# Gelu images of a Fourier mixer transformed as half precision pairs, written in place, with the low part formed on GpSimd

## The chip, the cores and the metric

The kernel runs on one core of a Trainium2 chip. The metric is the device time of one execution in microseconds; lower is better. The engines are TensorE (PE; weight loads are shown as PEld), VectorE (DVE), ScalarE (ACT), GpSimd (POOL) and the DMA queue of SyncE (SP). Each runs its own list of instructions in order; semaphores (`wait_ge`, `then_inc`) are all that ties them together.

## The reference, cut to what matters

The input is 4 x 32 images of 128 x 128 in float32. A Fourier neural operator layer (group norm, attention over tokens with spectral convolutions, two spectral mixer layers) is followed by a token attention and a mixture of experts. The change lies in the first mixer layer and in what feeds the second:

```python
m = instance_norm(attn, norm2_g, norm2_b)
m = fno_layer(m, mixer_w1, mixer_skip_w1, mixer_skip_b1, (H, W), norm=(mixer_norm_g1, mixer_norm_b1), act=_gelu)
m = fno_layer(m, mixer_w2, mixer_skip_w2, mixer_skip_b2, (H, W), norm=(mixer_norm_g2, mixer_norm_b2))
out = instance_norm(m, mixer_out_g, mixer_out_b) + attn
```

`fno_layer` adds a spectral convolution (forward transform, a product with weights on a few modes, inverse transform) to a pointwise skip path. So the gelu images of the first mixer layer are needed three times: their statistics, their forward transform for the second spectral convolution, and they themselves for the second skip path.

## The kernel before

There are 128 images; each lies in SBUF as 128 partitions (rows) by 128 elements. `m.b` holds the residual images, `m.a` a second set of images. `build` calls twelve stages in order, and each is a block with a barrier at its end. The change is in `stage_inverse(..., 'mix1')`, which the trace shows from about 328 to 446 us after its coefficients are turned and split; `stage_mixer` follows it and reads `m.half17` (the half transformed gelu images) and `m.stat`.

In `stage_inverse` the images are taken in 33 sets of up to 4 (`image_sets`, loop variable `b`; `width(b)` is 4 but for the last three sets, with 3, 3 and 2). Three sets form a quad `q` of 12 images, and `j` = 0, 1, 2 is the set's place in it. The engines' lists in 'mix1', per set:

- TensorE: `second(b)`, three half precision products that give the spectral rows of set b in a PSUM bank; `forward(b-2)`, for each image one float32 product of the gelu image (as weights) with the 34 columns of `dft17`, L1186; after each third set `first(q+2)`, twelve narrow half precision products for a later quad.
- VectorE: `linear(b+1)`, one tensor_scalar for each image from `m.b` into `m.tmp` (two places), L1296; it waits until the gelu of set b-1 has read its place. Then `combine(b)`, which adds the bank to `m.tmp`, L1330; `gelu_statistics(b-1)`, L1312; after each third set `half(q+2)`, L1281, the low part of the quad's half inverse, behind ScalarE's high part.
- ScalarE: the gelu of set b from `m.tmp` into the stage `m.ust` (two places, float32), L1263; `affine(b)`, which rescales the four images of `m.b` in place, L1237; `copied(b-2)`, which takes the forward product out of PSUM, L1228; after each third set `half(q+2)`, L1220.
- GpSimd: the add of the input images (loaded by SyncE into `m.a`) to `m.b`, L1142, behind `affine(b)`; then a copy of the gelu images from `m.ust` to `m.a`, L1145.
- SyncE: eleven loads of twelve images each into `m.a`, then the second mixer's weights.

The order of each list is written out by hand, as printed here:

Of the kernel before, what the change touches and what calls it, by code (L numbers as in the profile page):

```python
# [26 lines left out]
F16 = mybir.dt.float16  # L27
# [4 lines left out]
P = 128  # L32
# [138 lines left out]
def memory(nc, ctx, where):  # L171
# [3 lines left out]
    def sb(scope, name, shape, dtype=F32):  # L175
        return scope.enter_context(nc.sbuf_tensor(name, shape, dtype))
# [19 lines left out]
    with ExitStack() as l0:  # L196
        m.a = sb(l0, "images_a", [P, NI, NW])
        c0 = where['dft'][0]
        m.tab = sb(l0, "table", [P, where['var'][1] - c0])

        def tab(name, rows=P):
            lo, hi = where[name]
            return m.tab[0:rows, lo - c0:hi - c0]
        m.dft = tab('dft')
        m.dft17 = m.dft.rearrange("p (s k) -> p s k", s=2)[:, :, 0:K17]
        m.rows, m.cols, m.batch, m.low, m.var = tab('rows', FM), tab('cols', FM), tab('batch'), tab('low'), tab('var')
        pair = sb(l0, "pair", [P, 2, 2 * NM])
        m.wraw = pair[0:64, 0, :].rearrange("p (r k c) -> p r k c", r=ROWS, c=2)
        m.weff = pair[0:64, 1, :].rearrange("p (c m) -> p c m", c=2)
        m.feat = pair[:, 0, :].rearrange("p (x y) -> p x y", x=FM)  # L210
        m.coef = pair[:, 1, :].rearrange("p (x y) -> p x y", x=FM)
        mixw = sb(l0, "mixer_weights", [P, 2 * NM])
        m.mixw = mixw[:, :].rearrange("p (r k c) -> p r k c", r=ROWS, c=2)
        m.feat0 = mixw[:, :].rearrange("p (x y) -> p x y", x=FM)
        f = sb(l0, "features", [P, FQ * FQ])
        m.ft = f[:, :].rearrange("p (x y) -> p x y", x=FQ)
        m.half17 = f[:, 0:P * FM].rearrange("p (t x) -> p t x", t=P)
        g = sb(l0, "spare", [P, HC * P])
        m.spare = g[:, :]
        m.gramT = g[:, :].rearrange("p (c t) -> p c t", c=HC)  # L220
        m.coefH, m.coefL = (g[0:FM, 2 * NI * FM // 4 * i:2 * NI * FM // 4 * (i + 1)].bitcast(F16)
                            .rearrange("p (t x) -> p t x", t=NI) for i in (0, 1))
        m.modes = sb(l0, "modes", [P, 2, NM])
        r = sb(l0, "transposed", [P, 1920])
        m.turned = r[:, :]
        m.modesT = r[:, 0:1280].rearrange("p (k c t) -> p k c t", k=5, c=2)
        m.wT = r[:, 1280:1920].rearrange("p (k c h) -> p k c h", k=5, c=2)
        m.stat = r[:, 0:768].rearrange("p (t s) -> p t s", t=P)
        m.aff = r[:, 768:768 + 8 * P].rearrange("p (k t) -> p k t", k=8)
        m.halfH = sb(l0, "half_inverse_high", [P, 2, GRP * NW], F16)[0:3 * FM]  # L230
        m.halfL = sb(l0, "half_inverse_low", [P, 2, GRP * NW], F16)[0:3 * FM]
        m.rowsH = sb(l0, "rows_high", [P, 3, P], F16)[0:3 * FM]
        m.rowsL = sb(l0, "rows_low", [P, 3, P], F16)[0:3 * FM]
        m.colsH = sb(l0, "cols_high", [P, P], F16)[0:FM]
        m.colsL = sb(l0, "cols_low", [P, P], F16)[0:FM]
        m.unity = sb(l0, "unity", [P, P])[:, :]
        norms = sb(l0, "norms", [P, 160])
        m.norms = [norms[:, 32 * i:32 * i + 32] for i in range(5)]
        m.rstd, m.back = m.norms[3], m.norms[4]
        m.dftH = sb(l0, "transform_high", [P, FQ], F16)[:, :]  # L240
        m.dftL = sb(l0, "transform_low", [P, FQ], F16)[:, :]
        m.ust = shared[:, :].rearrange("p (s t w) -> p s t w", s=2, t=GRP)
        m.tmp = m.modes[:, :, 0:GRP * NW]

    b = m.b[:, :, :].rearrange("p a b -> p (a b)")
# [794 lines left out]
def stage_inverse(nc, held, m, kind, mix=None, ins=None):  # L1040


    s = semaphores(nc, held, "inverse_" + kind, "in0 in1 in2 in3 v sized rooted total scaled turned high low first bhigh "
                   "blow rows used lin ready saved forward copied weights cleared algebra affine added gstat partly")
    arrived = [s.in0, s.in1, s.in2, s.in3]
    sets = image_sets()
    up, down = m.col[:, 25:26], m.col[:, 26:27]
# [6 lines left out]
    def width(b):  # L1054
        return len(sets[b][2])
# [54 lines left out]
    with nc.Block() as block:  # L1110
# [22 lines left out]
        @block.gpsimd  # L1133
        def _(pool):
            if kind == 'proj':
                first_mixer(pool)
            if kind == 'mix1':
                for b in range(len(sets)):
                    q = sets[b][0]
                    pool.wait_ge(arrived[q % 4], 16 * (q // 4 + 1))  # L1140
                    pool.wait_ge(s.affine, b + 1)
                    pool.tensor_tensor(images(m.b, b), images(m.b, b), images(m.a, b), ALU.add).then_inc(s.added, 1)  # L1142
                    pool.wait_ge(s.added, b + 1)
                    pool.wait_ge(s.ready, b + 1)
                    pool.tensor_copy(images(m.a, b), m.ust[:, b % 2, 0:width(b)]).then_inc(s.saved, 1)  # L1145
            if kind == 'mix2':
                for b in range(len(sets)):
                    pool.wait_ge(s.lin, b + 1)
                    pool.tensor_tensor(images(m.b, b), images(m.b, b), images(m.a, b), ALU.add).then_inc(s.partly, 1)

        @block.tensor
        def _(pe):
# [26 lines left out]

            def forward(b):  # L1180

                pe.wait_ge(s.ready, b + 1)
                if b >= 2:
                    pe.wait_ge(s.copied, b - 1)
                for i in range(width(b)):
                    mm = pe.matmul(m.ps[6 + b % 2][:, i * FM:i * FM + FM], m.ust[:, b % 2, i, :], m.dft17,  # L1186
                                   start=True, stop=True)
                mm.then_inc(s.forward, 1)

            if kind == 'proj':  # L1190
# [23 lines left out]
        def _(act):  # L1214
# [7 lines left out]
                    e = act.copy(m.halfH[0:2 * FM, q % 2, whole:whole + NW], m.ps[q % 2][0:2 * FM, whole:whole + NW])  # L1222
                e.then_inc(s.bhigh, 1)

            def copied(b):
                act.wait_ge(s.forward, b + 1)
                n = width(b)
                act.copy(images(m.half17, b), m.ps[6 + b % 2][:, 0:n * FM].rearrange("p (t x) -> p t x", t=n))\  # L1228
                    .then_inc(s.copied, 1)

            def affine(b):

                q, j, gs = sets[b]
                store, k = (m.b, 0) if kind == 'mix1' else (m.a, 6)
                for i in range(len(gs)):
                    img = 12 * q + j + 3 * i
                    e = act.activation(store[:, img, :], store[:, img, :], ACT.Identity, scale=m.aff[:, k, img:img + 1],  # L1237
                                       bias=m.aff[:, k + 1, img:img + 1])
                e.then_inc(s.affine if kind == 'mix1' else s.lin, 1)
# [8 lines left out]
                act.activation(m.coefH[:, :, xs[0]:xs[0] + n], turned(r), ACT.Copy, scale=up[0:FM] if kind == 'proj' else 1.0).then_inc(s.high, 1)  # L1248
            half(0)
            half(1)  # L1250
            if kind == 'mix2':
                affine(0)
                affine(1)
            for b in range(len(sets)):
                if kind == 'mix2' and b + 2 < len(sets):
                    affine(b + 2)
                if kind == 'mix1':
                    act.wait_ge(s.used, b + 1)
                    if b >= 2:
                        act.wait_ge(s.forward, b - 1)  # L1260
                        act.wait_ge(s.saved, b - 1)
                        act.wait_ge(s.gstat, b - 1)
                    act.activation(m.ust[:, b % 2, 0:width(b)], spread(m.tmp[:, b % 2], width(b)), ACT.Gelu).then_inc(s.ready, 1)  # L1263
                    affine(b)
                    if b >= 2:
                        copied(b - 2)
                q, j, _ = sets[b]
                if j == 2 and q + 2 < QUADS:
                    half(q + 2)
            if kind == 'mix1':  # L1270
                copied(len(sets) - 2)
                copied(len(sets) - 1)

        @block.vector
        def _(vec):
# [31 lines left out]
            def gelu_statistics(b):  # L1307
                vec.wait_ge(s.ready, b + 1)
                q, j, gs = sets[b]
                for i in range(len(gs)):  # L1310
                    img = 12 * q + j + 3 * i
                    e = vec.bn_stats(m.stat[:, img, :], m.ust[:, b % 2, i, :])  # L1312
                e.then_inc(s.gstat, 1)

            def combine(b):
                vec.wait_ge(s.rows, b + 1)
# [33 lines left out]
            for b in range(len(sets)):  # L1350
                if kind == 'mix1' and b + 1 < len(sets):
                    linear(b + 1)
                combine(b)
                if b >= 1:
                    (gelu_statistics if kind == 'mix1' else statistics)(b - 1)
                q, j, _ = sets[b]
                if j == 2 and q + 2 < QUADS:
                    half(q + 2)
            (gelu_statistics if kind == 'mix1' else statistics)(len(sets) - 1)


def stage_factors(nc, held, m):
# [1135 lines left out]
```

## Time and profile before

| | |
|---|---|
| time, median of 3 runs | 2361.22 us (2359.89 to 2365.7) |
| the profiled execution's own time | 2359.8 us |
| its span | 2358.0 us |
| TensorE busy | 2084.6 us (88%) |
| VectorE busy | 1879.9 us (80%) |
| ScalarE busy | 1664.3 us (71%) |
| GpSimd busy | 601.8 us (26%) |
| mean granted TensorE clock | 0.905 of full speed |

The span is the time from the first to the last instruction; the execution's own time has 1.8 us more around it. A share of busy time is an average over twelve stages with different limits, so the stage that is changed has to be read by itself. In a timeline, neighbouring instructions of one line are merged (x4), and a bracket gives the idle time before them and what ended it; without a bracket there was practically none.

### The profile page before, as it was taken

The page shows a single profiled execution, that of the slowest core. Times are in us where ns is not written, and L with a number is a line of the kernel's source. Part 1 is how long each engine was busy: PE and PEld are TensorE (multiplying, and loading weights), DVE is VectorE, ACT ScalarE, POOL GpSimd, SP SyncE. Part 2 cuts the span into 40 slices and gives each one's busy share as a digit, 9 for nine tenths or more (in the row PEclk, how much of TensorE's full clock was granted, in tenths as well). Part 3 has the DMA queues.
Part 4 walks back from the last instruction along what each step waited for, and adds up shares of the span by engine and source line. Part 5 has one row for each costly group of instructions (what it writes and reads, how often), then busy time and mean ns, then how long its engine had stood idle before and what let it go on. Part 6 is the DMA issues. An engine that isn't in the chain of part 4 may idle for free. (4 is left out here: it accounts for less than half of the span.)

```text
span 2358.0 us, 30826 instructions
## 1 busy us (share of the span) xinstructions
PE 2084.6 (88%) x10373; PEld 1068.8 (45%) x10373; DVE 1879.9 (80%) x3566; ACT 1664.3 (71%) x2413; POOL 601.8 (26%) x751
## 2 busy tenths in 40 slices
PE   7776959874999999999999999999999999667778
PEld 7722446732444444444444444444444444323333
DVE  4667978688778888888889889888888888667776
ACT  1454236473788888888888888888888888566766
POOL 1035315345201202202202102102000000046768
PEclk9988655555999999999999999999999999788999
DMA  9003560000000000000000000000000000000101
GB/s 297 12 1 152 143 152 1 1 1 6 1 1 1 1 1 1 1 1 1 1 1 1 1 1 1 1 1 1 1 1 1 1 1 1 10 14 28 32 28 46
DMA packets 80833, 55.73 MB, mean 24 GB/s; under 512 B 11283, under 2 KB 78739, under 8 KB 79140
## 3 DMA queue, kind: packets, MB, share of 16 engines
q1 hardware_dynamic: 75476, 52.38, 7.4%
q10 hardware_dynamic: 5200, 1.38, 0.3%
q8 instruction: 83, 1.36, 0.2%
q14 instruction: 74, 0.61, 0.1%
HBM read 36.91 MB, written 16.78 MB: 23 GB/s over the span
## 5 line engine op out<-in xcount | busy, mean ns | idle before, releaser
L1912 ACT ACTIVATE inner<-banks,key_bias,scales 128x1024 f32<-128x1024 f32 x512 | 616.9, 1205 | 211.4 <-PE banks L1785 206.2
L2034 DVE TENSOR_TENSOR weights_low<-weights,weights_high 128x1024 f16<-128x1024 f32 x512 | 674.7, 1318 | 17.0
L1919 ACT ACTIVATE weights<-inner 128x1024 f32<-128x1024 f32 x512 | 541.1, 1057 | 16.1 <-DVE weights_low L2034 0.3
L2030 DVE CAST weights_high<-weights 128x1024 f16<-128x1024 f32 x512 | 371.5, 726 | 181.9 <-ACT weights L1919 169.1
L2108 POOL CAST sums_high<-sums 128x512 f16<-128x512 f32 x32 | 39.4, 1230 | 1091.3 <-ACT sums L1902 1073.3
L1785 PE MATMUL banks<-queries_high,keys_high 128*128 128x512 f16 x1024 | 304.5, 379 | 0.7 <-ACT inner L1912 0.7
L1800 PE MATMUL banks<-weights_high,tokens_low 128*128 128x512 f16 x1024 | 304.6, 379 | 0.0
L1785 PE MATMUL banks<-queries_low,keys_high 128*128 128x512 f16 x1024 | 304.6, 379 | 0.0
L1800 PE MATMUL banks<-weights_low,tokens_high 128*128 128x512 f16 x1024 | 304.5, 379 | 0.0
L1785 PE MATMUL banks<-queries_high,keys_low 128*128 128x512 f16 x1024 | 304.5, 379 | 0.0
L1800 PE MATMUL banks<-weights_high,tokens_high 128*128 128x512 f16 x1024 | 304.5, 379 | 0.0
L2289 ACT ACTIVATE scaled<-banks,gates 128x128 f32<-128x128 f32 x512 | 148.8, 394 | 85.3 <-PE banks L2236 78.8
L1800 PEld LDWEIGHTS banks<-weights_high,tokens_low 128*128 128x128 f16 x1024 | 100.2, 98 | 120.9
L1785 PEld LDWEIGHTS banks<-queries_low,keys_high 128*128 128x128 f16 x1024 | 100.2, 98 | 120.9
L1800 PEld LDWEIGHTS banks<-weights_high,tokens_high 128*128 128x128 f16 x1024 | 100.2, 98 | 120.8
L1800 PEld LDWEIGHTS banks<-weights_low,tokens_high 128*128 128x128 f16 x1024 | 100.2, 98 | 120.7
L1785 PEld LDWEIGHTS banks<-queries_high,keys_low 128*128 128x128 f16 x1024 | 100.2, 98 | 120.7
L2234 PE MATMUL banks<-expert_weights_high,normed_high 128*128 128x512 f16 x256 | 103.7, 405 | 50.3 <-DVE residual_and_scaled L2365 44.0
L1785 PEld LDWEIGHTS banks<-queries_high,keys_high 128*128 128x128 f16 x1024 | 96.9, 98 | 91.2 <-ACT inner L1912 1.7
L2429 POOL TENSOR_TENSOR scaled_halves<-scaled 128x256 f32<-128x256 f32 x128 | 93.4, 730 | 98.0 <-ACT scaled L2289 97.5
L2365 DVE SCALAR_TENSOR_TENSOR residual_and_scaled<-banks,gates,residual_and_scaled 128x128 f32<-128x128 f32 x384 | 110.0, 342 | 0.1
L2235 PE MATMUL banks<-expert_weights_low,normed_high 128*128 128x512 f16 x256 | 103.7, 405 | 0.0
(599 smaller groups left out, 3237.2 us busy)
## 6 DMA issues: line engine op xcount, KB each, us to landing
images_b<-in_x SPq DMA_DIRECT2D x32, 256.0 KB, 9.3
images_a<-in_x SPq DMA_DIRECT2D x8, 1024.0 KB, 10.3
mixed_scratch<-images_a SPq DMA_DIRECT2D x4, 2048.0 KB, 13.0
result<-group_result SPq DMA_DIRECT2D x32, 256.0 KB, 2.3
images_b<-mixed_scratch SPq DMA_DIRECT2D x10, 768.0 KB, 4.9
images_a<-in_x SPq DMA_DIRECT2D x10, 768.0 KB, 9.1
mixer_weights<-in_L_conv_mixer_w SPq DMA_DIRECT2D x4, 272.0 KB, 6.1
table<-tables ACTq DMA_DIRECT2D x1, 772.5 KB, 5.8
```

The lines of the kernel that those rows point to most:

```text
L1785: mm = pe.matmul(m.ps[2 * (t % 2) + h], key[:, par, part], query[:, q, 512 * h:512 * h + 512], start=(i == 0), stop=(i == 2))
L1800: mm = pe.matmul(m.ps[4 + h], value[:, par, k, :], weight[:, t % DEEP, 512 * h:512 * h + 512], start=(k == 0 and i == 0), stop=(k == KT - ...
L1912: act.activation(m.inner[:, t % 2, :], m.pair[t % 2], ACT.Exp, scale=m.fs[:, 1:2], bias=m.kb[:, c // QN % 2, k:k + 1]).then_inc(s.inner, 1)
L1919: act.activation(m.wt[:, t % 2, :], m.inner[:, t % 2, :], ACT.Exp).then_inc(s.outer, 1)
L2030: vec.tensor_copy(m.wH[:, t % DEEP, :], m.wt[:, t % 2, :]).then_inc(s.high, 1)
L2034: vec.tensor_tensor(m.wL[:, t % DEEP, :], m.wt[:, t % 2, :], m.wH[:, t % DEEP, :], ALU.subtract)\
L2108: after(pool.tensor_copy(m.oH[:, part], m.oS[:, part]))
L2234: pe.matmul(bank, m.lnH[:, t % RING, j, :], m.w8H[:, cols], start=True, stop=False)
L2235: pe.matmul(bank, m.lnH[:, t % RING, j, :], m.w8L[:, cols], start=False, stop=False)
L2289: o = act.activation(m.pb[:, n % 3, e, :], m.ps[ABANK[n % 2]][:, e * D:e * D + D], ACT.Copy, scale=m.gate[:, n, 4 + e:5 + e])
L2365: vec.scalar_tensor_tensor(out=m.u[:, n % 4, :], in0=m.ps[DBANK[n % 3]][:, e * D:e * D + D], scalar=m.gate[:, n, e:e + 1], in1=acc, op0=AL ...
L2429: pool.tensor_tensor(m.half[:, n % 2], m.pb[:, n % 3, 0:2], m.pb[:, n % 3, 2:4], ALU.add).then_inc(s.halved, 1)
```

## The change

The gelu image is now written to `m.a` in place of the input image (which GpSimd must have added to `m.b` before). ScalarE then copies it to half precision (`m.ustH`), GpSimd subtracts to get the low part (`m.ustL`), one set later in its list. TensorE's forward product becomes two half precision products for each image: the high part against the high and low table side by side (68 columns), and the low part against the high table (34 columns). VectorE, not ScalarE, takes the result out of PSUM and adds the two halves (`joined`), three sets later. The statistics read `m.a`. On ScalarE `affine(b+1)` now stands ahead of the gelu of set b and waits for `linear(b+1)`. The tables of the first transform, which were two tensors, lie in one.

```diff
--- before.py
+++ after.py
@@ -237,9 +237,12 @@
         norms = sb(l0, "norms", [P, 160])
         m.norms = [norms[:, 32 * i:32 * i + 32] for i in range(5)]
         m.rstd, m.back = m.norms[3], m.norms[4]
-        m.dftH = sb(l0, "transform_high", [P, FQ], F16)[:, :]
-        m.dftL = sb(l0, "transform_low", [P, FQ], F16)[:, :]
+        dfts = sb(l0, "transform_pair", [P, 2, FQ], F16)
+        m.dftH, m.dftL = dfts[:, 0, :], dfts[:, 1, :]
         m.ust = shared[:, :].rearrange("p (s t w) -> p s t w", s=2, t=GRP)
+        m.ustH, m.ustL = (shared[:, GRP * NW * i:GRP * NW * (i + 1)].bitcast(F16).rearrange("p (s t w) -> p s t w", s=2, t=GRP)
+                          for i in (0, 1))
+        m.dft17P = dfts[:, :, :].rearrange("p c (s k) -> p c s k", s=2)[:, :, :, 0:K17]
         m.tmp = m.modes[:, :, 0:GRP * NW]
 
     b = m.b[:, :, :].rearrange("p a b -> p (a b)")
@@ -1041,7 +1044,7 @@
 
 
     s = semaphores(nc, held, "inverse_" + kind, "in0 in1 in2 in3 v sized rooted total scaled turned high low first bhigh "
-                   "blow rows used lin ready saved forward copied weights cleared algebra affine added gstat partly")
+                   "blow rows used lin ready upper lower forward joined weights cleared algebra affine added gstat partly")
     arrived = [s.in0, s.in1, s.in2, s.in3]
     sets = image_sets()
     up, down = m.col[:, 25:26], m.col[:, 26:27]
@@ -1134,15 +1137,21 @@
         def _(pool):
             if kind == 'proj':
                 first_mixer(pool)
+            def below(b):
+                pool.wait_ge(s.upper, b + 1)
+                n = width(b)
+                pool.tensor_tensor(m.ustL[:, b % 2, 0:n], images(m.a, b), m.ustH[:, b % 2, 0:n], ALU.subtract)\
+                    .then_inc(s.lower, 1)
+
             if kind == 'mix1':
                 for b in range(len(sets)):
                     q = sets[b][0]
                     pool.wait_ge(arrived[q % 4], 16 * (q // 4 + 1))
                     pool.wait_ge(s.affine, b + 1)
                     pool.tensor_tensor(images(m.b, b), images(m.b, b), images(m.a, b), ALU.add).then_inc(s.added, 1)
-                    pool.wait_ge(s.added, b + 1)
-                    pool.wait_ge(s.ready, b + 1)
-                    pool.tensor_copy(images(m.a, b), m.ust[:, b % 2, 0:width(b)]).then_inc(s.saved, 1)
+                    if b:
+                        below(b - 1)
+                below(len(sets) - 1)
             if kind == 'mix2':
                 for b in range(len(sets)):
                     pool.wait_ge(s.lin, b + 1)
@@ -1179,12 +1188,13 @@
 
             def forward(b):
 
-                pe.wait_ge(s.ready, b + 1)
+                pe.wait_ge(s.lower, b + 1)
                 if b >= 2:
-                    pe.wait_ge(s.copied, b - 1)
+                    pe.wait_ge(s.joined, b - 1)
                 for i in range(width(b)):
-                    mm = pe.matmul(m.ps[6 + b % 2][:, i * FM:i * FM + FM], m.ust[:, b % 2, i, :], m.dft17,
-                                   start=True, stop=True)
+                    at = m.ps[6 + b % 2][:, 2 * i * FM:2 * i * FM + 2 * FM]
+                    pe.matmul(at, m.ustH[:, b % 2, i, :], m.dft17P, start=True, stop=False)
+                    mm = pe.matmul(at[:, 0:FM], m.ustL[:, b % 2, i, :], m.dft17P[:, 0], start=False, stop=True)
                 mm.then_inc(s.forward, 1)
 
             if kind == 'proj':
@@ -1222,16 +1232,12 @@
                     e = act.copy(m.halfH[0:2 * FM, q % 2, whole:whole + NW], m.ps[q % 2][0:2 * FM, whole:whole + NW])
                 e.then_inc(s.bhigh, 1)
 
-            def copied(b):
-                act.wait_ge(s.forward, b + 1)
-                n = width(b)
-                act.copy(images(m.half17, b), m.ps[6 + b % 2][:, 0:n * FM].rearrange("p (t x) -> p t x", t=n))\
-                    .then_inc(s.copied, 1)
-
             def affine(b):
 
                 q, j, gs = sets[b]
                 store, k = (m.b, 0) if kind == 'mix1' else (m.a, 6)
+                if kind == 'mix1':
+                    act.wait_ge(s.lin, b + 1)
                 for i in range(len(gs)):
                     img = 12 * q + j + 3 * i
                     e = act.activation(store[:, img, :], store[:, img, :], ACT.Identity, scale=m.aff[:, k, img:img + 1],
@@ -1248,6 +1254,8 @@
                 act.activation(m.coefH[:, :, xs[0]:xs[0] + n], turned(r), ACT.Copy, scale=up[0:FM] if kind == 'proj' else 1.0).then_inc(s.high, 1)
             half(0)
             half(1)
+            if kind == 'mix1':
+                affine(0)
             if kind == 'mix2':
                 affine(0)
                 affine(1)
@@ -1255,21 +1263,18 @@
                 if kind == 'mix2' and b + 2 < len(sets):
                     affine(b + 2)
                 if kind == 'mix1':
+                    if b + 1 < len(sets):
+                        affine(b + 1)
                     act.wait_ge(s.used, b + 1)
+                    act.wait_ge(s.added, b + 1)
+                    act.activation(images(m.a, b), spread(m.tmp[:, b % 2], width(b)), ACT.Gelu).then_inc(s.ready, 1)
                     if b >= 2:
                         act.wait_ge(s.forward, b - 1)
-                        act.wait_ge(s.saved, b - 1)
-                        act.wait_ge(s.gstat, b - 1)
-                    act.activation(m.ust[:, b % 2, 0:width(b)], spread(m.tmp[:, b % 2], width(b)), ACT.Gelu).then_inc(s.ready, 1)
-                    affine(b)
-                    if b >= 2:
-                        copied(b - 2)
+                    act.wait_ge(s.ready, b + 1)
+                    act.activation(m.ustH[:, b % 2, 0:width(b)], images(m.a, b), ACT.Copy).then_inc(s.upper, 1)
                 q, j, _ = sets[b]
                 if j == 2 and q + 2 < QUADS:
                     half(q + 2)
-            if kind == 'mix1':
-                copied(len(sets) - 2)
-                copied(len(sets) - 1)
 
         @block.vector
         def _(vec):
@@ -1309,8 +1314,16 @@
                 q, j, gs = sets[b]
                 for i in range(len(gs)):
                     img = 12 * q + j + 3 * i
-                    e = vec.bn_stats(m.stat[:, img, :], m.ust[:, b % 2, i, :])
-                e.then_inc(s.gstat, 1)
+                    vec.bn_stats(m.stat[:, img, :], m.a[:, img, :])
+
+            def joined(b):
+
+                vec.wait_ge(s.forward, b + 1)
+                n = width(b)
+                y = m.ps[6 + b % 2][:, 0:n * 2 * FM].rearrange("p (t c x) -> p t c x", t=n, c=2)
+                c.step(vec.tensor_scalar(images(m.half17, b), y[:, :, 0], 1.0 / P, None, ALU.mult))
+                vec.scalar_tensor_tensor(out=images(m.half17, b), in0=y[:, :, 1], scalar=1.0 / P, in1=images(m.half17, b),
+                                         op0=ALU.mult, op1=ALU.add).then_inc(s.joined, 1)
 
             def combine(b):
                 vec.wait_ge(s.rows, b + 1)
@@ -1353,10 +1366,15 @@
                 combine(b)
                 if b >= 1:
                     (gelu_statistics if kind == 'mix1' else statistics)(b - 1)
+                if kind == 'mix1' and b >= 3:
+                    joined(b - 3)
                 q, j, _ = sets[b]
                 if j == 2 and q + 2 < QUADS:
                     half(q + 2)
             (gelu_statistics if kind == 'mix1' else statistics)(len(sets) - 1)
+            if kind == 'mix1':
+                for b in range(len(sets) - 3, len(sets)):
+                    joined(b)
 
 
 def stage_factors(nc, held, m):
```

## Rows read from the trace of the kernel before

**Rows 1.** Busy time in a window: us, busy (x count) by engine, PEclk, DMA.

```profile
400.00:420.00 20.00, 19.10 (x86) 15.02 (x87) 15.82 (x50) 12.74 (x34) 11.27 (x12) 0.50 0.00 1
```

**Rows 2.** Waits from 340 to 440 us: total, times, longest.

```profile
ACT ow_stats_and_image_stage L1263 <- DVE modes L1330: 31.2, 19, 2.8
...
DVE half_inverse_low L1281 <- ACT half_inverse_high L1220: 16.7, 8, 2.1
PE banks L1186 <- ACT features L1228: 8.1, 9, 2.4
```

**Rows 3.** Timeline of ScalarE: start, us, what, [idle before <-releaser].

```profile
403.28 0.63 ACT L1263 ACTIVATE ow_stats_and_image_stage<-modes 128x512 f32<-128x512 f32 x1 [0.74 <-DVE modes L1330]
403.82 1.63 ACT L1237 ACTIVATE images_b<-images_b,transposed 128x128 f32<-128x128 f32 x4
...
405.51 0.58 ACT L1220 CAST half_inverse_high<-banks 102x512 f16<-102x512 f32 x1
...
414.37 0.63 ACT L1263 ACTIVATE ow_stats_and_image_stage<-modes 128x512 f32<-128x512 f32 x1 [0.75 <-DVE modes L1330]
```

**Rows 4.** Timeline of VectorE, the same stretch.

```profile
400.88 1.71 DVE L1296 TENSOR_SCALAR modes<-images_b,transposed 128x128 f32<-128x128 f32 x4
402.51 0.74 DVE L1330 SCALAR_TENSOR_TENSOR modes<-banks,small,modes 128x512 f32<-128x512 f32 x1
403.17 0.86 DVE L1312 BATCH_NORM_STATS2 transposed<-ow_stats_and_image_stage 128x6 f32<-128x128 f32 x4
406.12 0.69 DVE L1281 TENSOR_TENSOR half_inverse_low<-banks,half_inverse_high 102x512 f16<-102x512 f32 x1 [2.09 <-ACT half_inverse_high L1220]
...
409.49 1.11 DVE L1296 TENSOR_SCALAR modes<-images_b,transposed 128x128 f32<-128x128 f32 x4
```

**Rows 5.** Forward passes by line (busy us, mean ns), then a timeline of TensorE.

```profile
L1186 PE MATMUL banks<-table,ow_stats_and_image_stage 128*128 128x34 f32 x256 | 58.0, 395 | 10.0 <-ACT features L1228 8.9 <-ACT ow_stats_and_image_stage L1263 1.1
...
402.60 0.31 PE L1165 MATMUL banks<-cols_high,spare 34*102 34x128 f16 x1
402.70 0.31 PE L1163 MATMUL banks<-cols_high,spare 34*102 34x128 f16 x1
```

**Rows 6.** Timeline of GpSimd, the same stretch.

```profile
400.05 1.27 POOL L1142 TENSOR_TENSOR images_b<-images_b,images_a 128x512 f32<-128x512 f32 x1 [3.60 <-ACT images_b L1237]
401.38 0.61 POOL L1145 COPY images_a<-ow_stats_and_image_stage 128x512 f32<-128x512 f32 x1
...
405.60 1.27 POOL L1142 TENSOR_TENSOR images_b<-images_b,images_a 128x512 f32<-128x512 f32 x1 [1.13 <-ACT images_b L1237]
```

**Rows 7.** Timelines of VectorE, each cut to a single instruction.

```profile
400.88 0.52 DVE L1296 TENSOR_SCALAR modes<-images_b,transposed 128x128 f32<-128x128 f32 x1
...
401.33 0.75 DVE L1296 TENSOR_SCALAR modes<-images_b,transposed 128x128 f32<-128x128 f32 x1
```

**Rows 8.** Timeline of ScalarE in the attention stage.

```profile
999.00 1.21 ACT L1912 ACTIVATE inner<-banks,key_bias,scales 128x1024 f32<-128x1024 f32 x1 [0.63 <-PE banks L1785]
1000.24 1.06 ACT L1919 ACTIVATE weights<-inner 128x1024 f32<-128x1024 f32 x1
```

**Rows 9.** Groups by line: busy us, mean ns, idle before.

```profile
L2110 POOL TENSOR_TENSOR sums_low<-sums,sums_high 128x512 f16<-128x512 f32 x32 | 46.3, 1448 | 19.7 <-DVE weights_low L2034 18.4
...
L2098 POOL TENSOR_TENSOR tokens_low<-centred,tokens_high 128x508 f16<-128x508 f32 x30 | 34.7, 1157 | 35.6 <-DVE weights_low L2034 34.9
...
L1498 DVE TENSOR_SCALAR pair<-banks 128x128 f32<-128x128 f32 x1 | 0.3, 292 | 6.5 <-PE banks L1479 6.5
```

**Rows 10.** Timelines of VectorE and ScalarE, start and end of the stage.

```profile
328.45 2.14 DVE L1296 TENSOR_SCALAR modes<-images_b,transposed 128x128 f32<-128x128 f32 x8
...
327.82 1.28 ACT L1263 ACT_TABLE_LOAD   x1
331.28 0.63 ACT L1263 ACTIVATE ow_stats_and_image_stage<-modes 128x512 f32<-128x512 f32 x1 [2.17 <-DVE modes L1330]
...
442.90 0.41 ACT L1263 ACTIVATE ow_stats_and_image_stage<-modes 128x256 f32<-128x256 f32 x1
...
446.00 1.28 ACT L1489 ACT_TABLE_LOAD   x1 [0.29 <-PEq L1110]
```

## Prediction

> **What bounds the kernel now.** I read the page for the place of the stage, then for the stage `mix1` (328 to 446 us) the busy time in windows, the waits, and one third of a quad at a time in the timelines of VectorE, ScalarE and GpSimd. The windows [rows 1] show TensorE busy 19.10 of 20 us at half clock (0.50, the 1.2 GHz level), VectorE 15.82, ScalarE 12.74. Read alone, that says TensorE is the bound, and this change halves its forward products and more. The waits [rows 2] say otherwise: ScalarE's gelu waits 31.2 us for VectorE, VectorE's `half` waits 16.7 us for ScalarE, and TensorE itself waits 8.1 us for a ScalarE copy. Two engines that wait for each other in turn form a loop. The timelines close it. The gelu of the third set of a quad starts at 403.28 and that of the next quad at 414.37 [rows 3]: 11.09 us for three sets. Of these, ScalarE holds 403.28 to 406.09 (gelu 0.54, four affines 1.54, copy, `half` 0.58), and VectorE everything from 406.12 to the next gelu, 8.25 us, with no idle bracket on its later rows [rows 4]. 2.84 + 8.25 = 11.09: no TensorE instruction is in it. So TensorE's saving (8 float32 passes per set at 58.0/256 = 0.23 us each, 1.8 us, become 8 half precision ones of about 0.11 us, the spacing of the narrow products, 402.60 to 402.70 [rows 5]) is worth nothing unless this loop goes.
>
> One more thing of the present loop counts. VectorE's `linear` (four 128x128 tensor_scalars) takes 1.11 us at 409.49 and 1.71 at 400.88 [rows 4]. In the second case GpSimd is at work: add 400.05 to 401.32, copy 401.38 to 401.99 [rows 6]. Single instructions [rows 7]: the first ends at 401.40, the second runs 401.33 to 402.08. Each ended 0.08 us after the end of one GpSimd instruction. One tensor_scalar is held for the whole of each GpSimd instruction that it meets; GpSimd's own durations don't move, and neither do combine and the statistics. The Trainium skill, "SBUF — State Buffer", section "Who interferes with whom", calls this an exclusive lock on a port pair that GpSimd shares with VectorE's two-port modes; the trace agrees.
>
> **The change, part by part.** Write G, L, A, K for gelu, linear, the four affines and the new half precision copy. New order on ScalarE: A(b+1), G(b), K(b), and A(b+1) now waits for L(b+1), since the code adds that wait. L(b+1) still waits for G(b-1), because `tmp` has two places. So a chain that did not exist before closes on itself once per set: G(b-1), L(b+1), A(b+1), G(b). Before, A stood behind G and overlapped VectorE.
>
> Its length, with time 0 at the end of G(b-1):
> - L could start at 0.03. GpSimd's Add(b) starts when A(b) ends plus 0.15 (405.45 to 405.60 [rows 3, 6]). A(b) ends 0.54 before 0 (four affines last 1.63, the gelu starts 1.54 after their start and lasts 0.63). So Add runs from -0.39 to 0.88.
> - K starts 0.03 after G (ScalarE waits on itself that long: 1000.21 to 1000.24 [rows 8]) and takes about 0.63, as the gelu of the same shape. Its signal reaches GpSimd at 0.66 + 0.15 = 0.81, before Add is done.
> - GpSimd's new subtraction therefore follows Add at once, 0.94, for 1.15 us (`tokens_low`, same kind, 128x508 [rows 9]), to 2.09. The copy it replaces took 0.61.
> - L: the first instruction is held to 0.96, the second to 2.17, two more need 0.51 (402.08 to 402.59 [rows 4, 7]): L ends at 2.68.
> - A starts at 2.72, G at 4.26, and ends at 4.89.
>
> So 4.89 us a set against 11.09/3 = 3.70. VectorE's other work fits under A and G: from 2.60 (an instruction starts some 0.08 before the one ahead ends), combine 0.66, statistics 0.78 and the two new PSUM reads `joined` (0.29 was a 128x128 read of banks [rows 9]; for 136 elements, with the wait between, 0.60 together) end at 4.64. If `joined` were free nothing changes; if each half of it cost 0.74, the 128x512 read of combine [rows 4], the next L would start 0.6 late, but still behind Add's hold until 0.96, so also nothing. ScalarE loses the 0.25 us copy; not on the chain.
>
> Every third set (9 times) VectorE's `half` waits for ScalarE's, which now stands behind K: ready at 1.2, done at 1.81. The first tensor_scalar is then held until 2.17 all the same, three follow at 0.27: L ends 2.97 rather than 2.68, +0.29.
>
> **Sum.** Before, first to last gelu start is 442.90 - 331.28 = 111.62 us [rows 10]. After: the first period has no early subtraction in its way, about 4.2; then 27 of 4.89 = 132.0; 9 x 0.29 = 2.6; the last periods, with fewer images in L, A and G (an image less takes 0.25, 0.39 and 0.11 from them), and the last with a gelu behind K alone, an estimated 4.3 + 4.0 + 3.3 + 1.2 = 12.8. Together 151.6, so +40.0. Start: G(0) ran at 331.28; now L(0) 329.5, A(0) and A(1) to 332.8, the table load of 1.28 that stood in idle time [rows 10] falls behind them, G(0) at 334.1: +2.8. End: K, subtraction, product and `joined` of the last set follow each other (0.41, 0.44, 0.15 + 0.66, 0.4, 0.6 and signals between), about 2.9 us, against 3.1 us now from the last gelu at 442.90 to the next stage at 446.00 [rows 10]: nothing. Subtraction order (one set later on GpSimd), the joined semaphores, the moved tables: hidden, since TensorE gets its input two sets late. If that cover were gone, TensorE would wait, but it has 4.89 us a set for 1.28 + 0.86 + 0.44. Total +42.8 on 2359.8 (span 2358.0 and 1.8 around it) = 2402.6; the median of the runs stood 1.4 above that execution: 2404 us.
>
> Bounds. The subtraction: 1.15, or 1.45 as `sums_low` under VectorE's load [rows 9]: +0.3 x 30 = +9, 2413. Downward: the margin by which the subtraction catches the port is thin. It is ready at 0.81, could start at 0.94, and the second tensor_scalar wants the port at about 0.9; hence the second rival.
>
> **Rivals.**
> *VectorE wins the port.* If K ends only 0.15 us later than I say, the second to fourth tensor_scalars run first, at 0.28 each, L ends at 1.77, the period is 3.98, and the subtraction waits until 1.77. Thirds of a quad with `half` keep 5.18. 27 x 3.98 + 9 x 1.2 + 3.6 for the first + 11.5 for the last four = 133.4, which is 21.8 over 111.6, and 2.8 at the start: 2386. For it: the thin margin. Against it: the second tensor_scalar is recorded as started at 401.33, before GpSimd's 401.38, and was held all the same [rows 6, 7]. The Trainium skill (same section) says whichever starts first gets the pair; read by recorded starts that would give this rival.
> *The half precision subtraction doesn't hold VectorE* (nothing here shows this form against a tensor_scalar): L 1.11 to 1.4, period 3.35, with `half` 5.13: 27 x 3.35 + 9 x 1.78 + 3.35 + 10.5 = 120.4, so +8.8 + 2.8, 2373. Still slower, as the chain itself is new.
> *TensorE is the bound after all (faster).* From 19.10 of 20 us [rows 1]; 33 x 0.9 us saved would give 2332. It decides only where VectorE and ScalarE make a set in less than TensorE's present 3.5 us (1.3 for `second`, 1.8, 0.4 for `first`); the 11.09 us loop without TensorE speaks against it, and so does A behind L.
> *More contention* than the lock (GpSimd and VectorE both slowed, subtraction near 1.45): 2413 and above.
>
> **Numbers.** Main case 0.62 (own range 2397 to 2412), VectorE wins 0.15, no hold 0.08, more contention 0.11, TensorE bound 0.04. Range 2380 to 2419: below it lie the no-hold case and the faster one, above it a tail of contention. Faster by over 0.3% 0.04; within 0.3% (7 us, about what runs of this kernel can tell from nothing) 0.03; slower 0.93.
>
> **What would show it.** Right: gelu to gelu 4.9 us; four tensor_scalars of about 2.6 us, one of them over 1.1; ScalarE's affines waiting for VectorE's `linear` about 2 us a set; GpSimd instructions back to back; TensorE busy some 50 to 60% of the stage. Wrong: tensor_scalars under 1.8 us a set (second rival), gelus under 3.4 us apart, or TensorE still over 90% busy.

## The result, and the profile after

The new kernel takes 2400.59 us (median of 4 runs, 2399.59 to 2402.16) against 2360.55 us of the kernel before in the same comparison: ratio 1.0167, 95% interval 1.0153 to 1.0181. It is slower by 40.0 us; 2404 was forecast. The profiled span grows from 2358.0 to 2399.0 us.

The window of the new kernel that answers to [rows 1]:

```profile
400.00:420.00 20.00, 10.69 (x77) 5.65 (x78) 17.15 (x45) 12.02 (x27) 9.97 (x9) 0.50 0.00 1
```

TensorE has shrunk from 19.10 to 10.69 of 20 us at the same half clock, and the time went up. VectorE is now the busiest engine, 17.15 of 20, but part of that is time in which a GpSimd instruction holds one of VectorE's, as the rows below show. The waits of 340 to 480 us:

```profile
PE banks L1196 <- DVE features L1325: 75.1, 27, 6.0
POOL images_b L1151 <- ACT images_b L1243: 71.8, 29, 2.8
ACT images_b L1243 <- DVE modes L1301: 53.2, 29, 2.0
DVE half_inverse_low L1286 <- ACT half_inverse_high L1230: 12.2, 8, 2.0
...
DVE modes L1301 <- ACT images_a L1270: 5.6, 19, 0.8
```

TensorE now waits 75 us for VectorE's `joined`, without anybody waiting for TensorE. New against [rows 2] is the third line: ScalarE's affines wait 53.2 us, 29 times, for VectorE's `linear` (L1301). Before they waited for nothing. ScalarE's timeline (columns as in [rows 3]); L1243 are the affines, L1270 the gelu, L1274 the half precision copy:

```profile
404.27 0.61 ACT L1270 ACTIVATE images_a<-modes 128x512 f32<-128x512 f32 x1
...
407.86 1.65 ACT L1243 ACTIVATE images_b<-images_b,transposed 128x128 f32<-128x128 f32 x4 [1.78 <-DVE modes L1301]
409.41 0.61 ACT L1270 ACTIVATE images_a<-modes 128x512 f32<-128x512 f32 x1
410.12 0.63 ACT L1274 ACTIVATE ow_stats_and_image_stage<-images_a 128x512 f16<-128x512 f32 x1
412.66 1.65 ACT L1243 ACTIVATE images_b<-images_b,transposed 128x128 f32<-128x128 f32 x4 [1.91 <-DVE modes L1301]
414.21 0.61 ACT L1270 ACTIVATE images_a<-modes 128x512 f32<-128x512 f32 x1
```

The gelus at 409.41 and 414.21 are 4.80 us apart, and the one with VectorE's `half` in it, 404.27 to 409.41, is 5.14. VectorE over the same stretch:

```profile
406.11 0.69 DVE L1286 TENSOR_TENSOR half_inverse_low<-banks,half_inverse_high 102x512 f16<-102x512 f32 x1 [1.46 <-ACT half_inverse_high L1230]
406.71 1.11 DVE L1301 TENSOR_SCALAR modes<-images_b,transposed 128x128 f32<-128x128 f32 x4
...
410.06 2.56 DVE L1301 TENSOR_SCALAR modes<-images_b,transposed 128x128 f32<-128x128 f32 x4 [0.27 <-ACT images_a L1270]
412.54 0.74 DVE L1343 SCALAR_TENSOR_TENSOR modes<-banks,small,modes 128x512 f32<-128x512 f32 x1
...
413.98 0.28 DVE L1324 TENSOR_SCALAR features<-banks 128x136 f32<-128x136 f32 x1
414.29 0.30 DVE L1325 SCALAR_TENSOR_TENSOR features<-banks,features 128x136 f32<-128x136 f32 x1
414.86 2.56 DVE L1301 TENSOR_SCALAR modes<-images_b,transposed 128x128 f32<-128x128 f32 x4 [0.27 <-ACT images_a L1270]
```

and GpSimd (L1151 the add, L1143 the new subtraction):

```profile
405.73 1.15 POOL L1143 TENSOR_TENSOR ow_stats_and_image_stage<-images_a,ow_stats_and_image_stage 128x512 f16<-128x512 f32 x1
409.65 1.27 POOL L1151 TENSOR_TENSOR images_b<-images_b,images_a 128x512 f32<-128x512 f32 x1 [2.77 <-ACT images_b L1243]
410.87 1.15 POOL L1143 TENSOR_TENSOR ow_stats_and_image_stage<-images_a,ow_stats_and_image_stage 128x512 f16<-128x512 f32 x1
414.45 1.27 POOL L1151 TENSOR_TENSOR images_b<-images_b,images_a 128x512 f32<-128x512 f32 x1 [2.42 <-ACT images_b L1243]
415.67 1.15 POOL L1143 TENSOR_TENSOR ow_stats_and_image_stage<-images_a,ow_stats_and_image_stage 128x512 f16<-128x512 f32 x1
```

`linear` takes 2.56 us in the sets without `half`, where [rows 4] had 1.11 to 1.71, and it ends 0.60 after the subtraction: 410.87 + 1.15 = 412.02, and 412.62. Two of its four instructions, cut out singly, show the hold:

```profile
414.86 0.94 DVE L1301 TENSOR_SCALAR modes<-images_b,transposed 128x128 f32<-128x128 f32 x1 [0.27 <-ACT images_a L1270]
```

```profile
415.72 1.19 DVE L1301 TENSOR_SCALAR modes<-images_b,transposed 128x128 f32<-128x128 f32 x1
```

The first ends at 415.80, 0.08 us after the add's 415.72. The second ends at 416.91, 0.09 after the subtraction's 416.82. Both are the pattern of [rows 7], with the long subtraction in the copy's place. I call such a stretched instruction held, and say "port" for what VectorE and GpSimd can't use at once here; the rows show the hold, not the port itself.

Start and end of the stage, which answer to [rows 10]:

```profile
330.65 2.13 DVE L1301 TENSOR_SCALAR modes<-images_b,transposed 128x128 f32<-128x128 f32 x8
```

```profile
331.80 3.19 ACT L1243 ACTIVATE images_b<-images_b,transposed 128x128 f32<-128x128 f32 x8 [1.78 <-DVE modes L1301]
335.00 1.28 ACT L1270 ACT_TABLE_LOAD   x1
336.30 0.63 ACT L1270 ACTIVATE images_a<-modes 128x512 f32<-128x512 f32 x1
```

```profile
485.37 0.42 ACT L1270 ACTIVATE images_a<-modes 128x256 f32<-128x256 f32 x1
...
488.59 1.28 ACT L1507 ACT_TABLE_LOAD   x1 [2.30 <-PEq L1113]
```

From the first `linear` to the first gelu it is 5.65 us (2.83 before), the table load now standing behind eight affines. From the first to the last gelu, 485.37 - 336.30 = 149.07 us (111.62 before). From the last gelu to the next stage 3.22 (3.10 before). Together 157.94 against 117.55: +40.4 us in this stage. The stage begins 2.2 us later than before, and 1.6 us of that are made up after it. Such a shift also stands between executions with the same work up to there (the first `linear` starts at 328.45 in the kernel before and at 331.46 in the second experiment), so nothing is read from it.

### The profile page after: what moved, and what is told of

It reads as the page before. It is cut to its first block and busy times, and to the rows that moved or that the text cites. A ratio compares the mean times of both kernels' runs of the same rounds, so it can differ in the third digit from the quotient of the medians.

```text
span 2399.0 us, 30861 instructions
## 1 busy us (share of the span) xinstructions
PE 2047.5 (85%) x10373; PEld 1021.3 (43%) x10373; DVE 1917.6 (80%) x3632; ACT 1679.5 (70%) x2413; POOL 618.5 (26%) x751
```

## The experiments

All are compared with the kernel before on the same chip. Lines are those of each kernel.

**Subtraction behind linear.** In the new kernel:

```diff
                     if b:
+                        if b + 1 < len(sets):
+                            pool.wait_ge(s.lin, b + 2)
                         below(b - 1)
```

> The new kernel, where GpSimd's subtraction also waits for the next linear, so that only the add can hold VectorE's tensor_scalars. Chain and hold together (the prediction): linear ends at about 1.75 instead of 2.6 us, a set takes 3.9 to 4.0 us instead of 4.80, the nine sets with half stay at 5.1; 19 normal periods x 0.85 = 16 us less, 2384 us. If the hold by the subtraction isn't in the chain: 2400 us as the new kernel.

Measured: 2383.89 us, ratio 1.0090 (1.0073 to 1.0106). VectorE and GpSimd:

```profile
405.73 1.70 DVE L1303 TENSOR_SCALAR modes<-images_b,transposed 128x128 f32<-128x128 f32 x4 [0.27 <-ACT images_a L1272]
```

```profile
403.57 1.16 POOL L1143 TENSOR_TENSOR ow_stats_and_image_stage<-images_a,ow_stats_and_image_stage 128x512 f16<-128x512 f32 x1 [0.94 <-DVE modes L1303]
405.32 1.26 POOL L1151 TENSOR_TENSOR images_b<-images_b,images_a 128x512 f32<-128x512 f32 x1 [0.59 <-ACT images_b L1245]
407.51 1.15 POOL L1143 TENSOR_TENSOR ow_stats_and_image_stage<-images_a,ow_stats_and_image_stage 128x512 f16<-128x512 f32 x1 [0.93 <-DVE modes L1303]
```

`linear` is down to 1.70 us: the add, 405.32 to 406.58, still holds one instruction, the subtraction starts only at 407.51. The sets are 3.95 us apart. So of the 40 us that the new kernel is slower, some 17 are the hold by the subtraction. This edit also builds the order of the rival *VectorE wins the port*: 3.98 us a set and 2386 us were forecast for it.

**TensorE's relief alone.** In the kernel before, with constant weights, so that the transform of the gelu images is left out:

```diff
-                    mm = pe.matmul(m.ps[6 + b % 2][:, i * FM:i * FM + FM], m.ust[:, b % 2, i, :], m.dft17,
-                                   start=True, stop=True)
+                    at = m.ps[6 + b % 2][:, i * FM:i * FM + FM]
+                    pe.matmul(at, m.rowsH[:, 0, :], m.dft17H, start=True, stop=False)
+                    mm = pe.matmul(at, m.rowsH[:, 1, :], m.dft17H, start=False, stop=True)
```

> The kernel before, with TensorE's relief alone: two narrow half precision products for each image in place of the float32 one, with constant weights from the rows table (so the transform of the gelu images is left out). If the VectorE-ScalarE loop bounds the stage: no change, 2360 us within 0.2%, TensorE busy falls from 19 to about 14 of 20 us. If TensorE is the bound: 0.9 us x 33 = 30 us less, 2331 us.

Measured: ratio 0.9998 (0.9989 to 1.0007), with TensorE's busy time down:

```profile
400.00:420.00 20.00, 11.32 (x86) 5.88 (x87) 16.00 (x52) 14.75 (x38) 9.74 (x11) 0.50 0.00 0
```

TensorE is busy 11.32 of 20 us instead of 19.10 (about 14 was expected), and no gain is seen: from first to last gelu the profile has 111.59 us (334.29 to 445.88), against 111.62 before. A busy share near 100% was no bound.

**Four places for linear's result.** In the new kernel, with two unused stretches of another tensor as places three and four:

```diff
-                if b >= 2:
-                    vec.wait_ge(s.ready, b - 1)
+                if b >= 4:
+                    vec.wait_ge(s.ready, b - 3)
```

> The new kernel with four places for linear's result instead of two, so that linear no longer waits for the gelu of the set before: the chain is broken and the port stays shared. Chain theory: VectorE's own list sets the pace, linear 1.1 to 2.6 by how it meets GpSimd, plus 2.04 and half 0.2: about 3.5 to 4.2 us a set, 2362 to 2380 us. If the hold alone sets the pace (linear 2.56 every time), 4.8 us a set remain: 2397 to 2400 us.

Measured: 2400.27 us, ratio 1.0162 (1.0145 to 1.0178): the same as the new kernel, within the scatter of the runs. My expectation of 2362 to 2380 us missed, and with it one leg of the predicted chain. VectorE, then GpSimd:

```profile
408.24 2.91 DVE L1301 TENSOR_SCALAR modes<-images_b,transposed 128x128 f32<-128x128 f32 x4
411.07 0.74 DVE L1343 SCALAR_TENSOR_TENSOR modes<-banks,small,modes 128x512 f32<-128x512 f32 x1
...
413.04 2.91 DVE L1301 TENSOR_SCALAR pair<-images_b,transposed 128x128 f32<-128x128 f32 x4
```

```profile
408.17 1.27 POOL L1151 TENSOR_TENSOR images_b<-images_b,images_a 128x512 f32<-128x512 f32 x1 [2.77 <-ACT images_b L1243]
409.40 1.15 POOL L1143 TENSOR_TENSOR ow_stats_and_image_stage<-images_a,ow_stats_and_image_stage 128x512 f16<-128x512 f32 x1
412.97 1.27 POOL L1151 TENSOR_TENSOR images_b<-images_b,images_a 128x512 f32<-128x512 f32 x1 [2.42 <-ACT images_b L1243]
```

`linear` does start 0.3 us earlier, no longer behind the gelu, but takes 2.91 us instead of 2.56: the same two GpSimd instructions hold it to the same moment. 408.24 to 413.04 is 4.80 us again. (Only the first two periods got shorter, 2.74 and 3.18 us instead of 4.20 and 4.80; from the third on nothing changed.) So the loop isn't closed by the two places but by the port: affines end, the add starts 0.14 later, the subtraction follows, the rest of `linear`, the next affines. In the new kernel's rows: 409.51, 409.65, 410.87, 412.02, 412.62, 412.66, and the affines' end at 414.31, which is 4.80 after 409.51. A second way through this loop is as long: affines, gelu, half precision copy (to 410.75), subtraction. No run separates the two.

**Float32 products in the new kernel.** The large half precision product of each image becomes the float32 one of before:

```diff
-                    pe.matmul(at, m.ustH[:, b % 2, i, :], m.dft17P, start=True, stop=False)
-                    mm = pe.matmul(at[:, 0:FM], m.ustL[:, b % 2, i, :], m.dft17P[:, 0], start=False, stop=True)
+                    pe.matmul(at[:, 0:FM], m.a[:, 12 * sets[b][0] + sets[b][1] + 3 * i, :], m.dft17, start=True, stop=True)
+                    mm = pe.matmul(at[:, FM:2 * FM], m.ustL[:, b % 2, i, :], m.dft17P[:, 0], start=True, stop=True)
```

> The new kernel with the large half precision product of each image replaced by the float32 product of before (the small one stays, and joined adds them without the right scale, so the transform is not the reference's): TensorE gets about 0.23 x 8 - 0.11 x 4 = 1.4 us more per set, 4.0 of 4.8. If TensorE is off the chain: 2400.6 within 0.1%. If TensorE's time counts at all in this stage: up to 46 us more, 2446 us.

Measured: 2401.78 us, ratio 1.0169 (1.0154 to 1.0184), the new kernel's own 1.0167. TensorE busy went from 10.69 back to 16.42 of 20 us in the window 400 to 420, for nothing.

**Add and subtraction behind linear.** In the new kernel:

```diff
                     pool.wait_ge(s.affine, b + 1)
+                    if b + 1 < len(sets):
+                        pool.wait_ge(s.lin, b + 2)
                     pool.tensor_tensor(images(m.b, b), images(m.b, b), images(m.a, b), ALU.add).then_inc(s.added, 1)
```

> The new kernel, where GpSimd's add and its subtraction both wait for the linear of the next set. After e3 the loop is read as: affine ends, add, subtraction, release of the port, rest of linear, next affine (through the port, not through the two places). With both behind linear, linear runs free (1.11 us) and that loop is cut; what is left is gelu, linear, affine, gelu, 3.35 us, plus the part of the subtraction that reaches into the next linear, 0.2 to 0.3: 3.5 to 3.7 us a set, half sets 5.1 as before: 2374 to 2379 us. If the wait for two places (the prediction's chain) were the limit at 4.8: 2400 us.

Measured: 2374.56 us, ratio 1.0050 (1.0035 to 1.0065). VectorE:

```profile
401.07 1.17 DVE L1303 TENSOR_SCALAR modes<-images_b,transposed 128x128 f32<-128x128 f32 x4 [0.26 <-ACT images_a L1272]
402.15 0.74 DVE L1345 SCALAR_TENSOR_TENSOR modes<-banks,small,modes 128x512 f32<-128x512 f32 x1
...
404.47 1.17 DVE L1303 TENSOR_SCALAR modes<-images_b,transposed 128x128 f32<-128x128 f32 x4 [0.26 <-ACT images_a L1272]
```

`linear` runs free, 1.17 us, and the sets are 3.40 us apart. The bracket (0.26, for the gelu) is the wait through the two places. It stood in the new kernel too, but there the first instruction was then held past it. Here nothing is held, and the rows add up to the chain of the prediction, 3.35 us by its terms. It is hardly longer than VectorE's own list: in the next experiment, without the two places, the same sets still take 3.40 us. The sets with `half` stay at 5.15 us, which makes 11.95 a quad against 11.09 in the kernel before, and keeps this kernel above it.

**The same, with four places, and half later.** Added to the last one: the four places, and VectorE's `half` one set later:

```diff
-                if j == 2 and q + 2 < QUADS:
-                    half(q + 2)
+                if kind == 'mix1':
+                    if j == 0 and 1 <= q < QUADS - 1:
+                        half(q + 1)
+                elif j == 2 and q + 2 < QUADS:
+                    half(q + 2)
```

> As e5, with four places for linear's result, and VectorE's half one set later in its list, where ScalarE's part is long done. No chain and no half wait should be left; VectorE's own list (1.11 + 0.66 + 0.78 + 0.57 + 0.2 = 3.3 us, plus what it is held) sets the pace, 3.3 to 3.7 us for all sets: 32 x 3.5 = 112 us from first to last gelu against 149, 2363 us; 2357 at the short end, 2369 at the long. If half periods stay at 5.1: 2376 us.

Measured: 2357.69 us, ratio 0.9973 (0.9962 to 0.9985), the short end of what was expected. The window:

```profile
400.00:420.00 20.00, 13.69 (x90) 6.42 (x90) 19.79 (x65) 16.93 (x37) 13.48 (x13) 0.50 0.01 2
```

VectorE is busy 19.79 of 20, and from 340 to 436 us no wait of VectorE is listed: its own list is the bound. In this order the new kernel is 0.27% faster than the one before. But the next kernel, in the same comparison, gets 0.67% from the `half` edit alone. A quad takes 10.40 us here (gelus at 400.22 and 410.62) and 10.06 there (400.17 and 410.23). So VectorE's list with the new work on it is longer than TensorE's was without relief. Most of the new work is `joined`; `linear` takes 4.14 us a quad against 3.94. What each is worth was not measured apart.

**Half later alone, in the kernel before.** The same edit of `half`, nothing else.

> The kernel before with one edit: in mix1 VectorE's half stands one set later in its list, so that it doesn't wait 2.1 us for ScalarE's. If the loop of 11.09 us that I read in the prediction bounds the stage, it opens, and TensorE (about 10.1 us a quad) becomes the bound: 0.8 to 1.0 us x 10 less, 2351 to 2353 us. If TensorE already was the bound: 2361 us, no change.

Measured: 2347.57 us, ratio 0.9933 (0.9918 to 0.9948).

```profile
400.00:420.00 20.00, 20.00 (x89) 15.56 (x88) 18.03 (x58) 14.89 (x40) 11.39 (x13) 0.50 0.01 2
```

Now TensorE is busy 20.00 of 20 (90.00 of 90 from 340 to 430 us), and the next experiment shows that this time it counts. The gain is 16 us by these medians, and 12 in the repetition below, where 8 to 10 were expected; the profiled spans differ by 12.0 (2358.0 and 2346.0), of which 11.8 lie between first and last gelu (111.6 to 99.8).

**Half later, with TensorE's relief.** The same on the kernel of the second experiment.

> As e7 with the cheap half precision products of e2 (constant weights, the transform of the gelu images left out). If the loop hid TensorE's saving, it shows now: VectorE at about 8.9 to 9.3 us a quad becomes the bound, about 20 us less than the kernel before, 2340 to 2344 us. If TensorE's saving is worth nothing even then: as e7.

Measured: 2342.87 us, ratio 0.9917 (0.9898 to 0.9935).

```profile
400.00:420.00 20.00, 12.57 (x87) 4.61 (x86) 20.00 (x68) 17.46 (x46) 11.80 (x13) 0.50 0.01 2
```

TensorE's relief is worth something only now, about 5 us. By the medians alone that isn't certain, since the two intervals overlap; but from first to last gelu the profiles have 94.8 us, against 99.8 in both profiles of the kernel without relief. VectorE then sets the pace, busy 20.00 of 20 (80.00 of 80 from 340 to 420 us).

**Half later, again, and in all three inverse stages.**

> The same kernel as e7, timed again beside the next one on one chip: 0.993 of the kernel before, 2347 us.

> As e7 in all three inverse stages, proj and mix2 too. In those two stages VectorE waits only a few us for ScalarE's half in the kernel before (24.7 us of such waits over all, most of them in mix1), so little is to be had: 0 to 4 us less than e7. It could lose where TensorE's rows then wait for a later half.

Measured: 0.9946 (0.9934 to 0.9959), slightly less gain than the 0.993 expected, and 0.9939 (0.9927 to 0.9952). That the edit in `mix1` is faster holds twice; whether the other two stages add to it stays open, the difference of 2 us is inside the intervals.

**The subtraction twice.** In the new kernel, the first result going to an unused place:

```diff
+                pool.tensor_tensor(m.twice[:, b % 2, 0:n], images(m.a, b), m.ustH[:, b % 2, 0:n], ALU.subtract)
                 pool.tensor_tensor(m.ustL[:, b % 2, 0:n], images(m.a, b), m.ustH[:, b % 2, 0:n], ALU.subtract)\
                     .then_inc(s.lower, 1)
```

> The new kernel with GpSimd's subtraction done twice (the first result goes to an unused place). If the loop runs through the port (affine, add, subtraction, rest of linear, affine), each set gets longer by the 1.15 us of the second subtraction less the tensor_scalar that the added hold replaces at the tail, 0.9 to 1.15: 28 sets, 2426 to 2432 us. If GpSimd's work were hidden and linear's wait for the gelu were the limit: 2401 us.

Measured: 2427.84 us, ratio 1.0283 (1.0267 to 1.0299). VectorE and GpSimd:

```profile
407.73 3.41 DVE L1303 TENSOR_SCALAR modes<-images_b,transposed 128x128 f32<-128x128 f32 x4 [0.27 <-ACT images_a L1272]
```

```profile
407.32 1.27 POOL L1153 TENSOR_TENSOR images_b<-images_b,images_a 128x512 f32<-128x512 f32 x1 [2.42 <-ACT images_b L1245]
408.54 1.15 POOL L1144 TENSOR_TENSOR pair<-images_a,ow_stats_and_image_stage 128x512 f16<-128x512 f32 x1
409.65 1.15 POOL L1145 TENSOR_TENSOR ow_stats_and_image_stage<-images_a,ow_stats_and_image_stage 128x512 f16<-128x512 f32 x1
```

`linear` takes 3.41 us instead of 2.56, three of its instructions held in turn, by add and two subtractions. The normal sets are 5.65 us apart (gelus at 407.08 and 412.73): of the 1.15 us added on GpSimd 0.85 arrive in the period, as expected, because the hold takes the place of one instruction of `linear`, about 0.3 us. So GpSimd's work is on the path, though GpSimd is busy only 11.91 of 20 us.

## Why the prediction was right

**The bound before.** Right. The loop of VectorE and ScalarE, 11.09 us a quad with no TensorE in it, was the bound: TensorE's relief alone gives 0.9998, and opening the loop at `half` gives 0.993 at once. In the new kernel TensorE can be loaded again without effect (the fourth experiment).

**The period.** 4.89 us forecast, 4.80 measured. Of the 0.09, the larger part is the handover on GpSimd: I had the subtraction start 0.06 after the add's end, as the copy did; it is recorded 0.05 before it (410.87 against 410.92). The rest is the gelu, 0.61 instead of 0.63, against a little more between affines. `linear` was to end 2.68 after the gelu and ends 2.60 after it (410.02, 412.62). The subtraction was priced at 1.15 and took 1.15; `joined` at 0.60 and takes 0.61 (413.98 to 414.59), off the path: the next `linear` still waits 0.27 us for the gelu. The signs that the prediction named also came: ScalarE's affines wait 53.2 us in 29 times, 1.8 each, and TensorE is busy 53% of the window.

**The sets with `half`.** 5.18 forecast, 5.14 measured, for a slightly wrong reason: I had one instruction held until 2.17. At 406.71 the subtraction (to 406.88) has only 0.17 left, less than an instruction lasts, so `linear` ran its free 1.11.

**The sum.** First to last gelu 151.6 forecast, 149.1 measured; 18 normal periods at 0.09 less and nine with `half` at 0.04 less are 2.0 of the 2.5, and the last four, 12.3 instead of 12.8, are the rest. Start +2.8 forecast, 5.65 - 2.83 = 2.8 measured. End nothing, 0.1 measured. The stage alone grew by 40.4 us where 42.8 was forecast.

**The chain.** Its members and its length came out, one leg of its explanation did not. The prediction closed it through the gelu and the two places of `tmp`. The third experiment removed that leg and changed nothing from the third period on; the leg that holds is affines, add, subtraction, port, and the last experiment lengthened it with the effect expected. That the number agreed is partly luck, as far as the named leg goes: it agreed because the prediction also worked out the hold from the end of the affines, and both ways round pass through the same `linear` and the same affines. The leg I named comes second: it adds up to 3.40 us a set when the port is free. That `affine` now waits for `linear` is common to both ways; no run takes this wait away by itself.

**The rivals.** *VectorE wins the port* (2386) fell: the second instruction was recorded as started at 415.72, the subtraction at 415.67, and it was held for all of it. But the margin was thinner than I wrote, and that it was enough is partly luck. The half precision copy started 0.10 us after the gelu, not 0.03, and ended 0.73 after it, not 0.66 (410.02, 410.75): half of the 0.15 that I gave it. The subtraction started 0.12 after the copy's end, and ScalarE's signal had taken 0.14 to reach GpSimd a moment before (409.51 to 409.65), so there was next to nothing to spare. No run moves the copy later; the price of the rival was about right, as the first experiment, which forces its order, took 3.95 us a set and 2383.89. *No hold* (2373) fell by the same rows; the fifth experiment, which keeps `linear` free, took 3.40 us a set and 2374.56, near that rival's 3.35 and 2373. *TensorE the bound* fell by two experiments. *More contention* did not come: 1.15 us each time, with VectorE the one that waits.

## What to carry to other kernels

A busy share of 95% doesn't make an engine the bound. Look for a loop of waits between two other engines that adds up to the period without the busy one. If there is one, a cheap edit may be to let one of the two do its part later: here one small edit gave 0.993 and 0.995, where cutting the busy engine's time from 19.10 to 11.32 of 20 us gave nothing. With the loop open the busy engine was a bound after all, so the order of the edits matters. Before work is put on GpSimd because it is idle, ask which VectorE instructions run beside it: here, in the sets without `half`, add and subtraction each held one tensor_scalar to their end, and with ScalarE's affines waiting for `linear` that hold lay on the path of each such set. When an explanation's number comes out, remove one leg of it anyway; here the period was right to 2% and the leg was not the one.

## What the runs showed of the hardware that was not expected

- The narrow half precision products were priced at 0.11 us each. At half clock, with 128x128 weights, pairs of 68 and 34 columns start every 0.08 us, and in a set of four images the next product, of another kind, starts 0.33 us after the first of the eight (409.94 and 410.27). The large products of one of the last sets, which has three images:

```profile
485.09 0.21 PE L1196 MATMUL banks<-transform_pair,ow_stats_and_image_stage 128*128 128x68 f16 x1 [2.06 <-DVE features L1325]
...
485.17 0.22 PE L1196 MATMUL banks<-transform_pair,ow_stats_and_image_stage 128*128 128x68 f16 x1
...
485.25 0.22 PE L1196 MATMUL banks<-transform_pair,ow_stats_and_image_stage 128*128 128x68 f16 x1
```

- Recorded starts do not always tell which instruction is held. In [rows 6, 7] a tensor_scalar recorded at 401.33 was held by a copy recorded at 401.38; in the new kernel one at 415.72 was held by the subtraction at 415.67. A held tensor_scalar ended 0.08 to 0.09 us after the GpSimd instruction for each of the three kinds seen here (float32 add, float32 copy, subtraction to half precision).
- GpSimd was not untouched in every run, as the prediction had it: in the half later kernel a copy that started at 403.81, with a tensor_scalar running from 403.67 to 404.02, took 0.68 us, and one that met none, at 409.49, took 0.61.
